# New turn order in a recurrent stage, with moved constants, roots and loads

## What is computed

```
n    = layernorm(x)                                   # [b, l, d]
beta = (n @ eW) / max(sum(adj, axis=2), 1e-7)[..., None]
agg  = einsum('blu,blm->bmu', beta, adj)
h_t  = tanh(agg[:, t] @ Wx + h_{t-1} @ Wh + b)        # 128 steps, one after another
x1   = x + h
z    = layernorm(x1)
top-2 of z @ gate_w + gate_b, softmax of the two
moe  = sum over the two experts of w * (relu(z @ w1[e] + b1[e]) @ w2[e] + b2[e])
out  = x1 + layernorm(z + moe) * gamma + beta
```

## Time and profile before

| what | us |
|---|---|
| median of 3 runs | 688.69 (687.42 to 689.32) |
| profiled execution, device time | 691.58 |
| its span | 689.8 |
| busy: PE, DVE, ACT, POOL | 528.7, 512.4, 413.4, 466.1 |
| busy DVE in 140 to 200 us | 58.6 of 60 |
| POOL scatters in the recurrent stage | 128, from 102.9 to 269.1 |
| TensorE clock granted, mean | 0.901 |

### The profile page before, as it was taken

How to read it: one execution, slowest core, us unless ns; L and a number is a source line. 1 busy time by engine, 2 the same in 40 slices (tenths; PEclk the granted TensorE clock), 3 DMA queues, 4 the chain that set the end, 5 groups by cost and what they waited for, 6 DMA issues and landing times. The chain is left out here.

```text
span 689.8 us, 17491 instructions
## 1 busy us (share of the span) xinstructions
PE 528.7 (77%) x4140; PEld 479.5 (70%) x4140; DVE 512.4 (74%) x2551; ACT 413.4 (60%) x1350; POOL 466.1 (68%) x526
## 2 busy tenths in 40 slices
PE   1767799799999610899999999700899999999950
PEld 1656577577777510799999999700899999989840
DVE  4999489799989850588888888600388988888980
ACT  2889556466655301466666666400688899889940
POOL 3666707777777774277777777775177777777775
PEclk9988899999999855699999999955799999999985
DMA  8999639533433131589866655341997667764110
GB/s 212 283 276 285 181 118 304 162 107 117 116 101 102 54 121 47 139 266 327 250 218 195 209 189 171 145 152 40 301 337 243 214 195 213 211 191 141 47 51 7
DMA packets 115096, 121.40 MB, mean 176 GB/s; under 512 B 19017, under 2 KB 99613, under 8 KB 115008
## 3 DMA queue, kind: packets, MB, share of 16 engines
q1 hardware_dynamic: 95936, 76.79, 40.1%
q0 software_dynamic: 17920, 43.03, 17.2%
q10 hardware_dynamic: 1152, 0.56, 0.3%
HBM read 68.67 MB, written 55.90 MB: 181 GB/s over the span
## 5 line engine op out<-in xcount | busy, mean ns | idle before, releaser
L224 POOL DMA_INDIRECT rows_by_second<-R x144 | 145.6, 1011 | 63.0 <-issue 35.4
L224 POOL DMA_INDIRECT out_dram<-R x144 | 142.4, 989 | 63.5 <-issue 36.9
L1043 PE MATMUL bank<-W,hs 128*128 x1152 | 176.7, 289 | 0.0
L1096 ACT ACTIVATE hs<-bank,wr 128x128 f32<-128x128 f32 x432 | 126.9, 365 | 73.3 <-PE bank L1027 67.4
L224 POOL DMA_INDIRECT rows_by_first<-st x128 | 126.1, 985 | 60.5 <-issue 33.2
L1027 PE MATMUL bank<-xT,wr 128*128 128x128 f32 x1152 | 159.0, 282 | 8.1 <-ACT xT L1077 8.1
L1043 PEld LDWEIGHTS bank<-W,hs 128*128 128x128 f32 x1152 | 152.3, 193 | 3.6
L1027 PEld LDWEIGHTS bank<-xT,wr 128*128 128x128 f32 x1152 | 143.1, 196 | 15.3 <-ACT xT L1077 15.3
L1168 DVE SCALAR_TENSOR_TENSOR R<-bank,R 128x128 f32<-128x128 f32 x288 | 86.9, 343 | 62.4 <-PE bank L1043 62.2
L1085 ACT COPY wr<-W1b 128x258 f32 x288 | 104.2, 421 | 0.0
L1016 PE MATMUL bank<-ident,R 128*128 128x128 f32 x288 | 45.1, 281 | 67.8 <-DMA R<-rows_by_second 40.7
(11 more groups left out here) (136 smaller groups left out, 825.4 us busy)
## 6 DMA issues: line engine op xcount, KB each, us to landing
R<-rows_by_second SPq DMA_DIRECT2D x144, 196.0 KB
R<-rows_by_first SPq DMA_DIRECT2D x144, 68.0 KB
xq<-in_x_dram SPq DMA_DIRECT2D x32, 256.0 KB, 4.3
aq<-in_adj_dram SPq DMA_DIRECT2D x32, 256.0 KB, 5.1
x2r<-in_x_dram SPq DMA_DIRECT2D x32, 256.0 KB, 2.8
rows_by_second<-filler SPq DMA_DIRECT2D x1, 3136.0 KB, 11.9
rows_by_second<-filler SPq DMA_DIRECT2D x16, 196.0 KB
rows_by_second<-R POOLq DMA_INDIRECT x144
```

What stands on the lines that cost most here:

```text
L224: return nc.gpsimd.indirect_dma_start(dst, bass.IndirectOffsetOnAxis(ap=idx, axis=0), src, None, bounds_check=limit[n], oob_is_err=False)
L1043: i = mm(o, hs[:, h, c, k * P:(k + 1) * P], W2[:, bass.ds(e[k], 1), c, :].rearrange("p o f -> p (o f)"), start=False, stop=c == 1, skip_gr ...
L1096: i = a(hs[:, h, c, k * P:(k + 1) * P], ps_h[c][h][:, k * P:(k + 1) * P], ACT.Relu, bias=wr[:, u % 2, 2 * h + k, F + c:F + c + 1])
```

## The change

1. DVE's turns: in `odd` and `even` the places come right behind `tile_a`, the gate after that; in `odd` `tile_b` and `tile_b2` go to the end, in `even` the chain of ten root operations stands alone at the end.
2. PE's side jobs: `turn_h` and `count` behind k = 0, `logits` behind k = 1, `fresh` behind k = 2, `turn_x` behind k = 3. The first input part is cut: one matmul of 128 columns, then one of 384.
3. ACT: `exps` and `sums` of a quad move from behind tanh 1 to behind tanh 0, `tokens` from behind tanh 0 to behind tanh 1; the first tanh reads the small matmul's result.
4. POOL: the constants stand ahead of the first root. Quads 0, 1, 30 and 31 get a root each (`single`) in place of two for a pair.
5. SP: the fill of `rows_by_second` in two halves behind the `x2r` loads of quads 11 and 15, `W1b` in two halves behind quads 19 and 23, b1, gamma and beta behind quad 27.
6. DVE: the split of b2 moves behind the tables that follow the last turn; PE waits for it (`s_b2s`) before the expert passes.

The core of the diff (the orders of the two turns and of `steps` stand below as rows; the b2 block is moved unchanged):

```diff
-            filled(dram_b.ap()[TAIL:ROWS, :], W_B, NE).then_inc(s_fill, 16)
-            sp.dma_start(W1b[:, :, 0:F], w1.rearrange("e h f -> h e f")).then_inc(r_w, 16)
...
-            with sp.Fori(2, NQ // UN) as J:
-                for u in range(UN):
-                    tiles(UN * J + u, u)
+            for q in range(2 * UN, NQ):
+                tiles(q, q % UN)
+                if q in (11, 15):
+                    h = (q - 11) // 4
+                    rows = TAIL + h * NE // 2 * P
+                    filled(dram_b.ap()[rows:rows + NE // 2 * P, :], W_B, NE // 2).then_inc(s_fill, 16)
+                if q in (19, 23):
...
+                if q == 27:
...
+            def single(q):
...
+                pool.wait_ge(s_st, q + 1)
+                g.tensor_tensor(sc[:, 1, 0:QUAD], mv[:, u, :, 1], eps_ln[:, 0:QUAD], ALU.add)
...
+                g.tensor_tensor(scq[:, u, :], sc[:, 3, 0:QUAD], mhalf[:, 0:QUAD], ALU.pow).then_inc(s_scq, 1)
...
-            quads(pool, scale, SLOTS)
             pool.wait_ge(s_row, 1)
...
             rest()
 
+            for q in (0, 1):
+                single(q)
+            for u in range(2, SLOTS):
+                scale(u, u)
+            with pool.Fori(1, NQ // SLOTS - 1) as J:
...
+            for q in (NQ - 2, NQ - 1):
+                single(q)
...
-            fresh(0, 0).then_inc(s_rn, 1)
+            mm(ps_xt[:, 0:P], Ec[:, :], AX[:, 0:1, :].rearrange("p o b -> p (o b)"), start=True,
+               stop=True).then_inc(s_rn, 1)
+            mm(ps_rnn[0][:, P:QUAD * P], Ec[:, :], AX[:, 1:QUAD, :], start=True, stop=True, skip_group_check=True)
```

More of the change, by code:

```diff
@@ L375, in _ @@
             rest()
+            for q in (0, 1):
[3 more added lines that the diff above has]
+            with pool.Fori(1, NQ // SLOTS - 1) as J:
+                for u in range(SLOTS):
+                    scale(SLOTS * J + u, u)
+            for q in range(NQ - SLOTS, NQ - 2):
+                scale(q, q % SLOTS)
+            for q in (NQ - 2, NQ - 1):
+                single(q)
             for q in range(NQ):
@@ L456, in steps @@
                            skip_group_check=True).then_inc(s_rn, 1)
-                    if k == 0 and not (isinstance(q, int) and q == NQ - 1):
-                        fresh(q + 1, u + 1)
-                    if k == 1 and beyond(q, 1):
-                        turn_h(q - 1, u - 1)
-                    if k == 1 and beyond(q, 2):
-                        logits(q - 2, u - 2)
-                    if k == 2 and beyond(q, 4):
-                        count(q - 4, u - 4)
-                    if k == 3 and beyond(q, 1):
+                    if k == 0 and q > 0:
+                        turn_h(q - 1, u - 1)
+                    if k == 0 and q > 3:
+                        count(q - 4, u - 4)
+                    if k == 1 and q > 1:
+                        logits(q - 2, u - 2)
+                    if k == 2 and q < NQ - 1:
+                        fresh(q + 1, u + 1)
+                    if k == 3 and q > 0:
                         turn_x(q - 1, u - 1)
@@ L474, in _ @@
             turn_h(NQ - 1, UN - 1)
+            count(NQ - 4, UN - 4)
             logits(NQ - 2, UN - 2)
-            count(NQ - 4, UN - 4)
             turn_x(NQ - 1, SLOTS - 1)
+            count(NQ - 3, UN - 3)
             logits(NQ - 1, UN - 1)
-            for n in range(3, 0, -1):
+            for n in range(2, 0, -1):
                 count(NQ - n, UN - n)
@@ L815, in odd @@
                 one(tile_a, t - 1)
-                one(tile_b, t - 1)
+                one(place_1, t - 4)
                 pair(gate_1, p)
-                one(tile_b2, t - 1)
+                one(place_2, t - 4)
                 pair(gate_2, p)
-                one(place_1, t - 4)
+                one(place_3, t - 4)
                 pair(gate_3, p)
-                one(place_2, t - 4)
                 pair(apart, p)
                 one(gate_4, t - 3)
-                one(place_3, t - 4)
                 one(gate_5, t - 3)
+                one(tile_b, t - 1)
+                one(tile_b2, t - 1)
             def even(t):
@@ L831, in even @@
                 one(tile_a, t - 1)
+                one(place_1, t - 4)
+                pair(soft_2, p - 1)
+                one(place_2, t - 4)
+                pair(soft_3, p - 1)
+                one(place_3, t - 4)
                 one(tile_b, t - 1)
```

82 lines of the change are left out of this document (46 added, 36 removed).

## The result

The changed kernel took 684.71 us (median of 6 runs, 683.27 to 685.78), the kernel before 687.74 in the same comparison (6 runs, 687.00 to 689.32): a ratio of 0.9945, 95% interval 0.9924 to 0.9967. So the gain is 3.0 us in the first comparison and 5.7 in the second, 3.8 and 5.4 by their ratios. The forecast was 684.3. The profiled execution of the changed kernel has a span of 684.0 where before had 689.8.

The account below looks back on a forecast made before the run. Outside the unchanged expert passes, POOL's 128 scatters were taken as the bound, hiding late recurrence work. Terms 0.5 - 0.9 - 2.6 - 1.4 = -4.4 us took the median from 688.69 to 684.3; range 682.3 to 687.6.

Parts of the forecast that it names:

- Term 1: Stage one: constants ahead of POOL's first root make the first factors late; +0.5 us (0 to +3.1).
- So 0.8 to 1.6 us late is mostly absorbed: Stage one: late factors reach DVE only through the ring of eight slots, where later loads find less queue; 0.5 us charged.
- The rival of 3.1 us: Stage one: full-cost four-column `pow`, delay handed on by the ring; ends 3.1 us later, 686.9 in all; chance 0.17.
- Term 2: Recurrence up to tanh 0 of quad 4: smaller first matmul and reordered PE jobs save time; -0.9 us (-0.2 to -1.6).
- the unknown that was allowed 0.7: PE's granted clock early in the recurrence: a low clock may hit other matmuls, worth up to 0.7 us either way.
- Term 3: DVE's first places, turn 4: the last place ends 2.75 us after tanh 0 of quad 4, not 5.35; -2.6 (-1.5 to -3.0).
- Term 4: POOL's gap at the 21st scatter goes, as SP's b1 loads no longer delay quad 8's x; -1.4 us (0 to -1.5).
- It holds SP as long: SP's queue: b1 behind quad 27's x still holds SP, 17.7 us with gamma and beta, without making quad 28's x late.
- What must not eat this: DVE's turns in the recurrence: two lengthen to 9.84 us, 4.92 per quad, still under POOL's 5.14, so POOL has no gap.
- No cost: Halved fill and `W1b` loads, and the b2 split beside late scatters: nothing charged; a documentation rule would make it up to 1.6 us.
- The signs: Trace marks expected, such as first scatter at about 99.9; wrong if POOL idles over 0.3 mid stage or first tanh passes 78.7.
- One rival: Stage one's delay vanishes and the full clock is granted through quad 1 of the recurrence: 682.8 us; chance 0.06.

Follow-up runs that it names:

- the control: The changed kernel run again with nothing altered, beside the kernel before: 683.49 us against 689.17, ratio 0.9921.
- The run with three clears: Changed kernel with POOL's constants behind the last root, plus three 128x256 clears in each of DVE's even turns 8 to 30: 688.60 us.
- the run with one small clear: Changed kernel with POOL's constants behind the last root, plus one 128x64 clear in each of DVE's even turns 8 to 30: 683.41 us.

## Why the prediction was right, point by point

The forecast was 4.4 us below 688.69, and the median came at 684.71, 4.0 below. The parts are +1.1, -0.9, -2.55 and -1.6, in sum -4.0. That the sum agrees so closely is luck. The kernel before had a median of 687.74 in the same comparison, so the gain was 3.0 us there and 5.7 in the second one; terms 1 and 2 are uncertain by about 1 and 0.5 us. The mark from the last scatter to the passes' first, for which nothing was forecast, is 0.5 shorter on average in the new order (19.3 in 11 traces for 19.8 in three), though the ranges overlap. What the runs do show is that each term has the sign and about the size forecast, except term 1.

**Term 1 (+0.5 forecast, +1.1 found).** The mechanism was right: POOL's constants delay the first factors, and this reaches DVE only through the ring of eight slots. The size was off. The `pow` took 1.05 us, not 0.85, and ACT's first `xs` began at 16.14, not 15.9; that is small. The step that failed is "So 0.8 to 1.6 us late is mostly absorbed". I compared with the paired roots of the kernel before, and so took the delay for about 1 us. Against single roots without the constants ahead of them it is 4.0 (14.02 for 10.02), of which the ring takes 2.1; the singles, worth about 0.8, give some of it back. By DVE's last statistics the loss is 1.4. The rival of 3.1 us was nearer in the first trace (+1.94), by chance of the loads and of the clock.

**Term 2 (-0.9 forecast, -0.9 found).** -0.64 for the split (0.6 forecast) and -0.25 to -0.70 for the rest, where 0.30 was forecast for two quads with `turn_h` and `logits` apart; the upper value holds a wait behind the split of b2, which the sum didn't have. The first pair of traces showed -2.27, which would have looked like a missed mechanism. It was the clock, the unknown that was allowed 0.7; it came to 1.4.

**Term 3 (-2.6 forecast, -2.55 found).** Turn 4 began 97.49 - 96.23 = 1.26 after tanh 0 of quad 4 (1.2 forecast), and the last place ended 2.80 after (2.75). That 1.08 of it would come without touching DVE's order was not in the working, though `turn_h` behind step 0 was named.

**Term 4 (-1.4 forecast, -1.6 found).** The gap is gone. But its price as a part of the change was underrated: had the new turn order come without it, the loss would have been 3.2 to 3.9. And one step was wrong without harm, "It holds SP as long". Behind quad 27 the two b1 loads held SP for 2.34 us, not 15.4 (SP's timeline, b1 and the next x):

```profile
198.54 2.34 SPq L290 DMA_DIRECT2D W1b<-in_L_ffn_b_dram  x2
...
203.43 0.33 SPq L259 DMA_DIRECT2D x2r<-in_x_dram  x1
```

They took 15.42, 15.62 and 16.36 only in the three traces in which they stood right behind the fill and `W1b` in one block, and 2.3 to 2.7 in the other eleven. What held SP there is not shown.

**What must not eat this.** Forecast 5.22 and 4.62, 9.84 for two; found 5.21 to 5.46 and 4.63 to 4.65 in most turns, so 9.84 to 10.10. No gap in mid stage. The sum of steps was right for the odd turn and up to 0.24 short in the even one. The mean over turns 6 to 30 is 9.99, so the slack under POOL's pace was 0.3 us in a pair, two thirds of the 0.44 forecast. Not in the working were pairs that take longer: 10.46 in the trace of after, 11.43 in the control, beside a TensorE that had a low clock for 6.8 us.

```profile
175.00:182.00 7.00, 7.00 (x32) 0.51 0.74 236
```

By then the places were about 4 us ahead of their scatters, and POOL showed no gap. The run with three clears shows that POOL's pace is the bound; it doesn't fix its place to a tenth, and the run with one small clear never came near it.

**No cost.** The b2 split (257.83 to 260.97) ran beside three scatters, and the longest, at 259.74, took 1.00 us for 0.97. By the rule of the Trainium skill, "SBUF — State Buffer", section "Who interferes with whom", it could have cost up to 1.6 (an estimate); the trace shows 0.03.

**The signs.** Last scatter ended at 264.57 (264.7 forecast) and row loads at 268.97 (269.1) were hit better than they deserved: stage one was 1.4 later than the forecast in that trace, and the recurrence 1.4 quicker. The first tanh at 79.53 was past the 78.7 that I had called a sign of being wrong. It was one, of term 1, and part of it was chance: the control had 77.45. DVE's idle time between 110 and 220 us was 1.3 us in twelve short pieces, and ACT had no wait on `rows_by_first`, as forecast. One rival was summed wrongly: stage one's delay gone (0.5) and 0.7 for the clock make 688.69 - 5.6 = 683.1, not 682.8, and either lies inside the forecast's own range.

## What to carry to other kernels

When one engine's serial work bounds a stage, what stands in front of its first piece is paid in full and what stands behind is free, but only to the slack that the other engines have left; an order that gets the first piece out sooner by lengthening every turn spends that slack, and stalls that were cheap before then cost more (POOL missed 1.4 and 1.6 us by one late tile under the old order, 2.5 and then 1.3 under the new). So price two edits together where one uses the slack that the other needs. Filling an engine's idle start with work is free only up to what the buffers behind it absorb, and a mark that moves between traces of one kernel is priced from several traces or not at all.

## What the runs showed of the hardware

GpSimd's `pow` on 128 partitions took 1.05 us for 4 columns and 1.67 for 8, so a root for four columns costs 0.63 of one for eight, not half. Its selects of 128x2048, which had slowed DVE's operation at line 791 to 1.97 us, left DVE's statistics alone: 0.87 us for four of them beside the selects, 0.87 without them (at 8.06 in the trace of after, at 8.18 in that of before). The split's cast at line 792 took 2.05 us beside the selects in the first trace of before, and 0.22 in the second, where it began just behind them. Two loads of b1 held SP's queue for 15.4 to 16.4 us right behind 5 MB of other transfers, and for 2.3 to 2.7 us elsewhere. The start of the recurrence moved by 2.1 us between two executions of one kernel; 1.3 of it is there at DVE's last statistics, the rest goes with a low clock behind them. The start of the passes moved by 1.6 us over all traces, in step with TensorE's granted clock behind its idle stretch: the clock rose 15.6 to 18.5 us after the last scatter's start, and the passes' first scatter followed 18.75 to 20.33 after it. In windows of the kernel before, then of after:

```profile
277.00:282.00 5.00, 2.67 (x11) 0.50 0.53 122
282.00:287.00 5.00, 5.00 (x27) 0.54 0.43 105
```

```profile
277.00:282.00 5.00, 5.00 (x35) 0.73 0.45 108
282.00:287.00 5.00, 5.00 (x48) 1.00 0.54 155
```

A clock of 0.50 is the 1.2 GHz level, 1.00 the 2.4 GHz level. After has its work there 4.5 us sooner, and its clock rises sooner too; why the rise comes at a different distance from the last scatter in different traces of the same instructions stays open.
